# One decoder layer with the Dynamic-Time-Warping attention on one core: which engine copies three kinds of results out of PSUM for the first batches

## What is computed

```
x = x + attn(layernorm(x))      # squared-score linear attention, 16 heads of 16
x = x + align(ctx, layernorm(x))# dynamic time warping path, expands the context's rows
x = x + ffn(layernorm(x))       # butterfly-mixed 256 -> 1024 -> 256 with gelu

# attn:  q, k, v = h @ Wq * 0.25, h @ Wk, h @ Wv
#        A[i, j] = (q_i . k_j)**2 for j <= i;  o = A v / (sum_j A + 1e-5);  o @ Wo
```

## Time and profile before

| | us |
|---|---|
| median of 3 runs | 913.97 |
| lowest and highest | 912.26, 914.85 |
| the profiled execution | 919.23 |
| its span, first to last instruction | 917.5 |

### The profile page before, as it was taken

How to read it: one execution, slowest core, us unless ns; L and a number is a source line. 1 busy time by engine, 2 the same in 40 slices (tenths; PEclk the granted TensorE clock), 3 DMA queues, 4 the chain that set the end, 5 groups by cost and what they waited for, 6 DMA issues and landing times.

```text
span 917.5 us, 12051 instructions
## 1 busy us (share of the span) xinstructions
PE 782.3 (85%) x3927; PEld 384.2 (42%) x3927; DVE 489.3 (53%) x1921; ACT 446.9 (49%) x672; POOL 147.5 (16%) x332
## 2 busy tenths in 40 slices
PE   4887988799899978899988978867899972699998
PEld 3352323234333324333233322334476561457657
DVE  5637553531546122569997884239759886431000
ACT  1245776766667754778865757523412300241220
POOL 2121222221221111212222202101001000100100
PEclk9899997889999989979999989977999986799999
DMA  4481532210323220314422211101010012000001
GB/s 145 146 251 65 184 108 77 69 48 23 116 70 149 71 59 20 89 34 137 132 90 84 61 39 34 25 9 28 15 38 31 15 45 64 10 0 24 24 0 46
DMA packets 52761, 61.25 MB, mean 67 GB/s; under 512 B 21007, under 2 KB 31939, under 8 KB 52699
## 3 DMA queue, kind: packets, MB, share of 16 engines
q1 hardware_dynamic: 51611, 56.28, 20.4%
q0 software_dynamic: 1088, 4.19, 1.4%
HBM read 37.16 MB, written 23.30 MB: 66 GB/s over the span
## 4 chain that ended last, share of the span: by engine, by line
PE 57%; DVE 29%; ACT 6%; issue 5%; DMA 2%; SPq 1%; DVEq 0%; ACTq 0%
PE psO L1205 11%; PE psS L1188 10%; PE psS L1352 8%; PE psW L1362 7%; PE psW L1257 5%; DVE FOLD L917 3%; DVE STATS L1032 3%; PE psW L1248 3%; PE psW L1280 3%; ACT ARENA L778 3%; DVE FOLD L977 3%; PE psW L1264 2%; PE psW L1289 2%; DVE XX L1053 2%; PE psW L1292 2%
## 5 line engine op out<-in xcount | busy, mean ns | idle before, releaser
L778 ACT ACTIVATE ARENA<-psS 128x1024 f32<-128x1024 f32 (+3 forms) x384 | 301.0, 811 | 110.5 <-PE psS L1188 107.7
L1188 PE MATMUL psS<-ARENA 96*128 96x512 bf16 (+3 forms) x768 | 196.2, 347 | 30.5 <-ACT ARENA L778 29.5
L702 POOL TENSOR_SCALAR_AFFINE_SELECT ARENA<-ARENA 128x256 f32<-128x256 f32 x256 | 110.4, 435 | 410.3 <-ACT ARENA L778 408.6
L1205 PE MATMUL psO<-ARENA 128*32 128x512 f32 (+3 forms) x1536 | 173.2, 525 | 3.4 <-ACT ARENA L783 2.5
L1188 PEld LDWEIGHTS psS<-ARENA 96*128 96x128 bf16 x768 | 57.1, 100 | 219.3 <-ACT ARENA L778 125.7
L1362 PE MATMUL psW<-W2E,ARENA 128*128 128x256 f32 x512 | 114.6, 385 | 6.8 <-DVE ARENA L1168 6.2
L1362 PEld LDWEIGHTS psW<-W2E,ARENA 128*128 128x128 f32 x512 | 98.7, 193 | 23.0 <-DVE ARENA L1168 6.6
L845 ACT ACTIVATE ARENA<-psS,BEFF 128x512 f32<-128x512 f32 x64 | 43.5, 687 | 122.7 <-PE psS L1352 122.7
L1248 PE MATMUL psW<-IDENT,XX 128*128 128x128 f32 x192 | 36.9, 348 | 46.8 <-DVE XX L1053 46.8
L1080 DVE TENSOR_TENSOR X<-X,psW 128x512 f32<-128x512 f32 x32 | 21.7, 684 | 100.6 <-PE psW L1280 50.6
L1257 PE MATMUL psW<-XX,ARENA 128*128 128x512 f32 x128 | 68.0, 638 | 5.1 <-DVE ARENA L1068 3.1
(11 more groups left out here) (143 smaller groups left out, 817.9 us busy)
## 6 DMA issues: line engine op xcount, KB each, us to landing
ARENA<-qk_parts SPq DMA_DIRECT2D x192, 128.0 KB, 2.7
qk_parts<-ARENA SPq DMA_DIRECT2D x16, 768.0 KB, 3.7
out<-ARENA SPq DMA_DIRECT2D x16, 256.0 KB, 2.1
X<-in_x POOLq DMA_DIRECT2D x3, 1024.0 KB, 7.2
dist<-ARENA SPq DMA_DIRECT2D x1, 2560.0 KB, 8.1
MORE<-dist SPq DMA_DIRECT2D x16, 160.0 KB, 2.3
path<-MORE SPq DMA_DIRECT2D x16, 80.0 KB, 2.0
path<-FOLD SPq DMA_DIRECT2D x16, 80.0 KB, 2.2
```

The costliest lines, as they stand in the source:

```text
L702: pool.affine_select(out=blk, in_=blk, compare_op=ALU.is_ge, fill=0.0, base=0, pattern=[[0, 2], [1, P]], channel_multiplier=-1).then_inc(s ...
L778: nc.scalar.activation(A[:, (2 * G + a) % A_PAIRS, :, 0:N], psS[:, a, :, 0:N], ACT.Square).then_inc(s_sq, 1)
L1188: ins = nc.tensor.matmul(psS[:, a, j, 0:N], KST[0:STACK, g % 2, 2 * a + j, kt * P:(kt + 1) * P], QST[0:STACK, g % 2, 2 * a + j, q0:q0 + N] ...
L1205: ins = nc.tensor.matmul(psO[32 * j:32 * j + 32, o % 2, q0 - qc * HALF:q0 - qc * HALF + N], V1[:, kt, GH * g + j], A[:, (2 * G + j // 2) % ...
```

## The change

For batches 0 to 2, VectorE copies the turned tiles of x and writes the first part of queries and keys; for batches 0 and 1 it copies the values, with one instruction of 512 columns for the two ScalarE ones of 256. The turned tiles and the values are copied with a plain copy, the first part with a multiplication by 0.25 or 1.0. Batch 3 stays as it was, and so do the values of batch 2. In each moved unit VectorE waits for TensorE's signal, and ScalarE has no instruction and no wait of it any more. The wait of `normal` is now at each even pair of tiles, for the two turned tiles that last read just this part of `XN`.

```diff
--- before.py
+++ after.py
@@ -232,15 +232,22 @@
 
     plan = make_plan()
     item_of = {u: k for k, u in enumerate(u for u in plan if u[0] in ITEM_KINDS)}
+    def by_vector(kind, b):
+
+        return kind in ("turn_x", "value", "qk") and b <= (1 if kind == "value" else 2)
+
     normals = [u for u in plan if u[0] == "normal"]
     normal_of = {u[1:]: k for k, u in enumerate(normals)}
+    tiles_of = {k: [u for u in normals if u[3] == k] for k in range(TT // 2)}
     turn_of = {"x": "turn_x", "student": "turn_s", "ffn": "turn_f"}
     hidden_of = {u[1:]: k for k, u in enumerate(u for u in plan if u[0] == "hidden")}
     out_of = {u[1:]: k for k, u in enumerate(u for u in plan if u[0] == "out")}
 
-    def last_turn(kind, b):
-
-        return max((u for u in plan if u[0] == turn_of[kind] and u[1] == b), key=plan.index)
+    def turned(kind, b, i):
+
+        of_pair = tiles_of[i]
+        k = of_pair.index(("normal", kind, b, i))
+        return max(ready(turn_of[of_pair[k - 1][1]], of_pair[k - 1][2], i // 2 * 2 + x) for x in range(2)) if k else 0
 
     def hidden_end(b, h):
 
@@ -752,12 +759,12 @@
                     _, what, b, t0, t1 = u
                     act.wait_ge(s_var, norm_of[u[1:]] + 1)
                     nc.scalar.activation(SD[:, t0:t1], VE[:, t0:t1], ACT.Sqrt).then_inc(s_sd, 1)
-                elif kind == "turn_x":
+                elif kind == "turn_x" and not by_vector(*u[0:2]):
                     _, b, i = u
                     h, k = i // 2, i % 2
                     act.wait_ge(s_ready, ready(*u))
                     nc.scalar.activation(XNT[:, k, h * HALF:(h + 1) * HALF], psW[:, bank(*u)], ACT.Copy).then_inc(s_free[bank(*u)], 1)
-                elif kind == "qk":
+                elif kind == "qk" and not by_vector(*u[0:2]):
                     _, b, i = u
                     m, s, h = i // 4, (i // 2) % 2, i % 2
                     if i == 0 and b:
@@ -776,7 +783,7 @@
                     if 2 * G + a >= A_PAIRS:
                         act.wait_ge(s_av, (2 * G + a - A_PAIRS) // 2 + 1)
                     nc.scalar.activation(A[:, (2 * G + a) % A_PAIRS, :, 0:N], psS[:, a, :, 0:N], ACT.Square).then_inc(s_sq, 1)
-                elif kind == "value":
+                elif kind == "value" and not by_vector(*u[0:2]):
                     _, b, i = u
                     act.wait_ge(s_ready, ready(*u))
                     for j in range(2):
@@ -998,7 +1005,7 @@
 
             for u in plan:
                 kind = u[0]
-                if kind in ITEM_KINDS and kind not in ON_SCALAR and not (kind == "up" and u[1] % 2 == 0):
+                if kind in ITEM_KINDS and (kind not in ON_SCALAR or by_vector(*u[0:2])) and not (kind == "up" and u[1] % 2 == 0):
                     dve.wait_ge(s_ready, ready(*u))
                     got, freed = psW[:, bank(*u)], s_free[bank(*u)]
                 if kind == "context":
@@ -1046,9 +1053,8 @@
                     settled()
                 elif kind == "normal":
                     _, what, b, i = u
-                    order = normal_of[u[1:]]
-                    if order and order % 4 == 0:
-                        dve.wait_ge(s_ready, ready(*last_turn(*normals[order - 1][1:3])))
+                    if turned(*u[1:]) and i % 2 == 0:
+                        dve.wait_ge(s_ready, turned(*u[1:]))
                     for t in (2 * i, 2 * i + 1):
                         ins = nc.vector.tensor_scalar(XN[:, t], X[:, b, t], MV[:, t, 0:1], RS[:, t:t + 1],
                                                       ALU.subtract, ALU.mult)
@@ -1062,6 +1068,8 @@
                         dve.wait_ge(s_dist_out[1][0], 16 * WAYS)
                         dve.wait_ge(s_dist_out[1][1], 16 * WAYS)
                     part = [QP[:, m, s, c, h * HALF:(h + 1) * HALF] for c in range(PARTS)]
+                    if by_vector(kind, b):
+                        nc.vector.tensor_scalar(part[0], psW[:, bank(*u)], 0.25 if s == 0 else 1.0, None, ALU.mult).then_inc(s_part1, 1)
                     dve.wait_ge(s_part1, b * 8 + i + 1)
                     if b or i:
                         dve.wait_ge(s_split, b * 8 + i)
@@ -1071,6 +1079,13 @@
                     vec(nc.vector.tensor_copy(part[1], R1))
                     settled()
                     nc.vector.tensor_tensor(out=part[2], in0=R1, in1=part[1], op=ALU.subtract).then_inc(s_split, 1)
+                elif kind == "turn_x" and by_vector(*u[0:2]):
+                    _, b, i = u
+                    h, k = i // 2, i % 2
+                    nc.vector.tensor_copy(XNT[:, k, h * HALF:(h + 1) * HALF], got).then_inc(freed, 1)
+                elif kind == "value" and by_vector(*u[0:2]):
+                    _, b, i = u
+                    nc.vector.tensor_copy(V1[:, 2 * i:2 * i + 2, :, 0:HD], got.rearrange("p (t h e) -> p t h e", t=2, h=NH)).then_inc(freed, 1)
                 elif kind == "products":
                     if u[2] in last_of:
                         heads_out(*u[1:])
```

## The result

| | before | changed |
|---|---|---|
| median of 15 runs | 913.97 us | 919.86 us |
| lowest and highest | 911.81, 916.81 | 916.80, 924.06 |
| profiled execution, its span | 919.23, 917.5 | 920.54, 918.6 |

The changed kernel is slower by a ratio of 1.0063, with a 95% interval of 1.0047 to 1.0079, that is 4.3 to 7.2 us. The forecast was 919.2. The two profiled executions are only 1.3 us apart, because the profiled one of before lies above all 15 timed runs of its kernel.

A forecast was written before the change was run, and what follows sets the result against it. VectorE was taken to bound batch 0 already, with the copies covered beside attention. Batch 0's 1.95 + 2.85 + 0.3 + 0.3 = 5.4, less 0.2, gave +5.2 on the median 913.97: 919.2 us, range 912.5 to 923.5.

The forecast's parts named there:

- The bound: VectorE already bounds batch 0's units of queries and keys; beside attention in batches 1 and 2 the moved copies are covered.
- The price of 0.69: Each moved copy on VectorE, all three kinds, takes 0.69 us; lower bound 0.46, upper 0.73.
- The sign at the first square: Attention's first square comes 5.4 us later than 59.95; the mechanism is wrong if under 3 us late.
- rival 1: Early in batch 0, PE's clock gives back up to 4.6 us, leaving +0.6: 914.6, no change; chance 0.2.
- Turned tiles, +1.95: Batch 0: turned tiles' copies queue behind VectorE's 14 reductions of `bits`, so `coef` starts 1.95 us later; bounds 1.8 to 2.2.
- First five units, +2.85: Batch 0's first five query and key units: period 1.98 becomes 2.67 us, 4 x 0.69 plus 0.09 for the first.
- The other three units, +0.3: Batch 0's three units alternating with `chain` find VectorE idle; each copy costs 0.09 us more; bounds 0 to 0.6.
- the values, +0.3: Batch 0: the last value copy stands ahead of biases and turned weights on VectorE, 0.27 us later; bounds 0.2 to 0.7.
- The lag behind it: After the first square both kernels stay in step, save 0.3 us around 250; a lag changing elsewhere would show error.
- Batches 1 and 2, -0.2: Batch 2's fourth turned tile 0.3 us sooner, batch 1's 0.09 later, the rest covered; bounds -16.5 to +1.
- 2: Between 60 and 290 us, ScalarE's queue bound PE; up to 16.5 us of waits return, -11, 903; chance 0.13.
- 3: Batch 0's units: PE falls to its lower level while waiting for VectorE, 3.1 us more, 922.3; chance 0.13.

The follow-up runs named there:

- b0_only: Only batch 0's moved copies on VectorE, batches 1 and 2 left on ScalarE, against the kernel before: 1.0063 (1.0042 to 1.0084).
- b12_only: Only the moved copies of batches 1 and 2 (turned tiles, first parts, batch 1's values) on VectorE, against the kernel before: 1.0030 (1.0011 to 1.0048).
- waits_only: No copy moved, only the wait of `normal` placed at each even pair, against the kernel before: 1.0003 (0.9985 to 1.0022).
- qk12_only: Only the first parts of batches 1 and 2 on VectorE, against the kernel before: 0.9991 (0.9967 to 1.0015).
- before_zero_early: The kernel before with the DMA that fills the distances issued earlier, no copy moved, against the kernel before: 0.9984 (0.9960 to 1.0009).
- best: The kernel before with the distances' fill issued early and only batch 2's turned tiles on VectorE, against the kernel before: 0.9971 (0.9948 to 0.9994), 911.89 us.
- after_zero_early: The changed kernel with the fill of the distances issued when the first turned tile is ready, against the kernel before: 1.0041 (1.0025 to 1.0056), 918.01 us.

## Why the prediction was right

**The bound: right.** Where the first parts lie beside attention they cost nothing that can be measured: 30.76 against 30.74 us from the second to the fourth heads, 0.9991 for them alone. Batch 0 alone brought as much as the whole change (1.0063 for b0_only). Against it stands b12_only, whose 1.0030 has no explanation; the two together would be more than the 1.0063 of the change.

**The price of 0.69: right** for all three kinds. The Trainium skill's ScalarE: Activation LUTs, section Rules for kernel authors, gives multiplying to VectorE, and gives its factor for bf16. Here, with fp32 read out of PSUM, VectorE's multiplication took 688 ns and ScalarE's 596, so the rule is no help; the 0.46 that stood beside it was the price of a cast that reads SBUF.

**The sign at the first square: not met as it stands.** The prediction said 5.4 us late, and the mechanism wrong under 3; the two profiles have 61.70 against 59.95, which is 1.75. The delays were there, but the clock took most of them back in this pair: 2.6 us by the low stretch, which only the kernel before has, and 0.5 by the first unit, of which the changed kernel does less at the lower level (4.07 us, for 4.54 in b0_only). That is rival 1, which had a chance of 0.2.

**Turned tiles, +1.95: right as a delay, wrong as a cost.** `coef` moved by 1.9 us in three of the four profiles with the gap (by 2.1 in the changed kernel, whose start is 0.2 late); the median moved by some 4.2. I had the early rise of the clock as something that could only give back time (rival 1). It is also a gain that the kernel before has in some executions, and that none of the four profiles with the gap has; that makes about 0.6 us on average, and the rest is open.

**First five units, +2.85: too large.** The period is 2.51 us and not 2.67: the copy of 25.93 is followed by one at 28.45 and by the next at 30.96, 33.48 and 35.99, so (35.99 - 25.93) / 4. The copy needs nothing of the third part ahead of it and starts as that ends; before, the rest started 0.1 after it. That makes 4 x 0.53 + 0.09 = 2.2.

**The other three units, +0.3, and the values, +0.3: right.** Between the fifth rest and the eighth 10.19 us became 10.48 where neither profile has a low stretch, and from the eighth rest to the first square 14.28 became 14.52 where the values are moved (b0_only). So all of batch 0 is 1.9 + 2.2 + 0.3 + 0.2 = 4.7 us at a like clock, for a forecast of 5.4. But the low stretch of the clock mostly goes away with the moved copies, so in the timed runs less of it is left.

**What I missed.** The first heads wait for the fill of the distances. Its issue is the last of SyncE's long queue of batch 0, which starts with the fourth unit's third part. The kernel before had 0.5 us to spare there (64.91 + 8.1 against 73.53), and I had looked only at what the scores need. The wait is 1.1 us in the profile of the changed kernel, of which nothing is left at the second heads.

**The lag behind it: it moves where no moved copy lies,** which the prediction had named as a sign of being wrong. Take the six profiles with all of batch 0 on ScalarE and no copy moved ahead of it (the kernel before, waits_only, b12_only, qk12_only, before_zero_early, best) and the three with all of it on VectorE behind `bits` (b0_only, the changed kernel, after_zero_early). Their means differ by 3.3 us at the first square, 3.1 at the second heads, 2.6 at the twelfth (272 us) and 5.5 at the end. Half of the lag at the end has come behind all moved copies. Most of that is between 550 and 650 us, in b0_only and the changed kernel and not in after_zero_early. The stretch in waits_only, the changed kernel and b0_only:

```profile
550.00:650.00 100.00, 78.23 (x346) 38.41 (x347) 49.51 (x191) 44.10 (x70) 12.80 (x21) 0.88 0.12 23
550.00:650.00 100.00, 78.39 (x331) 37.73 (x332) 45.83 (x176) 43.01 (x68) 12.59 (x21) 0.83 0.12 22
550.00:650.00 100.00, 77.85 (x323) 37.32 (x320) 44.23 (x171) 42.59 (x67) 12.60 (x21) 0.80 0.12 22
```

The granted clock is 0.88, 0.83 and 0.80, and 0.88 in after_zero_early. Whether batch 0's delay brings this about or chance does, nine profiles don't tell.

**Batches 1 and 2, -0.2: right.** The fourth turned tile of batch 2 was copied sooner:

```profile
251.08 0.69 DVE L1085 COPY XX<-psW 128x512 f32<-128x512 f32 x1 [0.20 <-PE psW L1263]
```

That answers to the earlier trace rows: 251.08 for 251.21, and the stretch around it took 24.24 us for 24.57.

So the forecast of 5.2 us met the 5.9 of the medians with a right place and a right price, but the nearness of the two numbers is luck. It had 0.7 too much for batch 0. The low stretch that goes away with the first parts costs 2.1 us on average over the eight profiles with these copies on ScalarE and 0.2 over the six with them on VectorE, so 1.9 are given back. Against that stand 0.6 for the early rise and at most 1.1 for the fill. These are estimates from the profiles, and with the 0.3 gained in batch 2 they make 3.1 to 4.2 us, under the measured interval of 4.3 to 7.2. What makes up the difference is open; the lag that appears between 550 and 650 us is the candidate. Of the rivals, 2 is refuted, as the waits for squares stayed, and 3 did not occur: between 34 and 42 us the granted clock is 1.00 in five of the six profiles with the longer period.

## What to carry to other kernels

Before a copy is moved to another engine, look at what stands ahead of it in that engine's queue: here 1.85 us of reductions that had been free cost, by the medians, more than the copies. Follow each queue that starts from the moved work to its last instruction, and ask who waits for that one; a DMA with half a microsecond to spare is the next bound. And where the clock of TensorE moves by execution, compare stretches between like events in several profiles, as two single executions can hide a loss of 0.6%.

## What the runs showed of the hardware

TensorE's granted clock goes with the spread between executions of the same kernel. Of 35 runs of the kernel before, the three shortest (910.4 to 911.9 us) had a mean granted clock of 0.934 to 0.936, the three longest (919.2 to 920.0) one of 0.927 to 0.929. In batch 0 alone it took the first square from 55.37 us (before_zero_early) to 59.95 (the kernel before) with the same work for the engines. The profile's clock column can't be trusted early in the kernel: in the kernel before it reads 1.00 from 0 to 24 us, though a query matmul takes 1061 ns until 24 us and 592 behind it. The durations have to be read there.
